# Running mean of the tokens on TensorE, phase biases as rows of a product, reciprocal of the positions first

## What is computed

```python
off_in = concatenate([x, pp], -1)                     # x: 4 x 512 x 64, pp: 512 x 32 phases
ao = (gelu(off_in @ hop_w1 + hop_b1) @ hop_w2 + hop_b2).reshape(B, L, H, P + 1)
center = tanh(ao[..., :P]) * PI                       # H = 4, P = 32
key_ph = tanh(x @ cpe_w + cpe_b) * PI
ctx = cumsum(x @ kce_w + kce_b, axis=1)
pos = arange(1, L + 1).reshape(1, L, 1)
storage_in = concatenate([x, ctx / pos], -1)          # ctx / pos: the running mean
st_ph = tanh(gelu(storage_in @ ksk_w1 + ksk_b1) @ ksk_w2 + ksk_b2) * PI
```

## Time and profile before

| | |
|---|---|
| median of 3 runs | 214.59 us (214.52 to 216.08) |
| the profiled execution's own time | 213.43 us |
| its span, first to last instruction | 211.7 us |
| TensorE products busy | 147.7 us (70%) |
| VectorE busy | 131.1 us (62%) |
| ScalarE busy | 73.9 us (35%) |
| GpSimd busy | 35.6 us (17%) |
| share of the chain that ended last | TensorE 43%, VectorE 34% |
| mean granted TensorE clock | 0.778 |

### The profile page before, as it was taken

How to read it: one execution, slowest core, us unless ns; L and a number is a source line. 1 busy time by engine, 2 the same in 40 slices (tenths; PEclk the granted TensorE clock), 3 DMA queues, 4 the chain that set the end, 5 groups by cost and what they waited for, 6 DMA issues and landing times.

```text
span 211.7 us, 2099 instructions
## 1 busy us (share of the span) xinstructions
PE 147.7 (70%) x690; PEld 90.8 (43%) x690; DVE 131.1 (62%) x342; ACT 73.9 (35%) x122; POOL 35.6 (17%) x52
## 2 busy tenths in 40 slices
PE   0889858029279694499581054877479989979992
PEld 0543524024175512458561053766454454534340
DVE  2659995789942898998879995388673005101011
ACT  2010511252233640784840230323063462444541
POOL 2031500346000472241402330000000000000000
PEclk9999979758857955558997555799555896799998
DMA  5999600000000000000000000000000000101011
GB/s 145 345 386 377 262 5 25 0 0 0 0 0 0 0 0 0 0 5 2 0 0 5 0 0 0 0 5 0 0 0 0 0 3 0 25 0 25 0 25 25
DMA packets 7042, 8.80 MB, mean 42 GB/s; under 512 B 2388, under 2 KB 4436, under 8 KB 7032
## 3 DMA queue, kind: packets, MB, share of 16 engines
q1 hardware_dynamic: 7032, 8.68, 12.2%
HBM read 8.15 MB, written 0.52 MB: 41 GB/s over the span
## 4 chain that ended last, share of the span: by engine, by line
PE 43%; DVE 34%; issue 9%; DMA 5%; ACT 5%; POOL 2%; SPq 1%; DVEq 0%; POOLq 0%; ACTq 0%
PE bank L900 8%; PE bank L884 6%; DMA dist_sb<-in_dist 5%; PE bank L885 4%; PE bank L861 2%; PE bank L640 2%; DVE dist_sb L988 2%; PE bank L705 2%; PE bank L698 2%; PE bank L702 2%; DVE proj L1059 2%; PE bank L707 2%; DVE invpos L993 2%; PE bank L690 2%; PE bank L754 1%
## 5 line engine op out<-in xcount | busy, mean ns | idle before, releaser
L586 ACT ACTIVATE hid<-bank 128x512 f32<-128x512 f32 x32 | 18.1, 596 | 23.3 <-PE bank L885 22.2
L900 PE MATMUL bank<-hid,ffn_sb 128*64 128x512 f32 x64 | 18.9, 676 | 0.0
L1271 DVE TENSOR_TENSOR h<-bank,h 128x256 f32<-128x256 f32 x4 | 1.7, 425 | 27.0 <-PE bank L909 27.0
L884 PE MATMUL bank<-xp,w1hi 128*128 128x512 f32 x32 | 16.6, 520 | 1.0 <-ACT xp L570 1.0
L885 PE MATMUL bank<-xp,w1lo 96*128 96x512 f32 x32 | 14.6, 455 | 0.0
L884 PEld LDWEIGHTS bank<-xp,w1hi 128*128 128x128 f32 x32 | 7.0, 220 | 14.4 <-ACT hid L586 8.1
L988 DVE TENSOR_TENSOR dist_sb<-dist_sb,mask_in 128x1024 f32<-128x1024 f32 x8 | 9.5, 1232 | 4.0 <-POOL mask_in L325 4.0
L698 PE MATMUL bank<-late_sb,proj 128*128 128x8 f32 x16 | 3.7, 364 | 10.8 <-ACT proj L469 10.8
L656 PE MATMUL bank<-early_sb,vk 128*128 128x128 f32 x8 | 2.2, 435 | 12.9 <-DVE vk L1038 12.9
L830 PE MATMUL bank<-early_sb,sq_c 128*128 128x2 f32 x16 | 2.9, 304 | 11.8 <-ACT sq_c L545 11.8
L640 PE MATMUL bank<-dist_sb,neigh 128*64 128x512 f32 x32 | 11.1, 775 | 0.0
(11 more groups left out here) (246 smaller groups left out, 369.4 us busy)
## 6 DMA issues: line engine op xcount, KB each, us to landing
dist_sb<-in_dist SPq DMA_DIRECT2D x4, 1024.0 KB, 10.8
mask_in<-in_mask SPq DMA_DIRECT2D x4, 256.0 KB, 10.0
ffn_sb<-in_ffn SPq DMA_DIRECT2D x1, 813.0 KB, 10.9
fold_sb<-in_folded SPq DMA_DIRECT2D x1, 772.0 KB, 12.1
late_sb<-in_late SPq DMA_DIRECT2D x1, 728.5 KB, 11.6
out<-h SPq DMA_DIRECT2D x8, 64.0 KB, 1.7
early_sb<-in_early SPq DMA_DIRECT2D x1, 391.0 KB, 3.2
mask_in<-in_mrows SPq DMA_DIRECT2D x1, 128.0 KB, 2.4
```

The lines of the kernel that those rows point to most:

```text
L586: nc.scalar.activation(hid[:, at % HB], bank[hid_bank[at % 3]][:, :], ACT.Gelu).then_inc(S["hid_set"], 1)
L884: nc.tensor.matmul(o, w1hi[:, e * HID:(e + 1) * HID], xp1[g][:, toks], start=True, stop=False)
L900: mm = nc.tensor.matmul(bank[2][j * D:(j + 1) * D, :], K["e_w2"][:, (e + j) * D:(e + j + 1) * D], hid[:, (at + j) % HB], start=False, stop ...
```

## The change

It makes the running mean on TensorE. A constant `run_mean` (128 x 4 x 128) holds, for each chunk c of 128 tokens, 1/position where the row's token is not later than the column's, and 0 elsewhere; GpSimd cuts it from `invpos` by an affine_select. cx is then summed in bank 3 straight from x, without its transpose: for each chunk c a product of x with the triangle of its own 128 columns, and one with `invpos` for all later columns (384, 256 and 128 of them). ScalarE copies the bank to cx. The scan and the multiply are gone. The biases of `center` and `st` become a product: a row of ones against a row of the bias, rounded to F32R in one row and its rest in another (rows 0 and 32 of 33), added in the bank in front of the fp32 product. ScalarE's tanh reads the banks, and three adds on VectorE per group are gone. The positions are written first and VectorE takes their reciprocal as its first instruction. GpSimd's two adds on x wait for the running mean. Banks 3 and 0 of the joint products change places. The late constants are shorter by one row block.

```diff
@@ gpsimd
+            nc.gpsimd.iota(invpos[:, :], [[1, L]], base=1, channel_multiplier=0,
+                           allow_small_or_imprecise_dtypes=True).then_inc(S["pos_set"], 1)
             nc.gpsimd.memset(ones[:, :], 1.0).then_inc(S["ones_set"], 1)
...
+            pool.wait_ge(S["inv_set"], 1)
+            nc.gpsimd.affine_select(out=run_mean[:], in_=invpos[:, :].rearrange("p (c t) -> p c t", t=P), compare_op=ALU.is_ge,
+                                    fill=0.0, base=0, pattern=[[0, NC], [1, P]],
+                                    channel_multiplier=-1).then_inc(S["run_set"], 1)
...
                 pool.wait_ge(S["x_set"], g + 1)
-                pool.wait_ge(S["xt_mm"], g + 1)
+                pool.wait_ge(S["cx_mm"], g + 1)
                 nc.gpsimd.tensor_tensor(v8(x[:, g]), v8(h[:, g]), v8(x[:, g]), ALU.add).then_inc(pool_step, 1)
@@ scalar, project
                 nc.scalar.copy(x_t[:, :], bank[0][:, :]).then_inc(S["xt_set"], 1)
                 yield
+                act.wait_ge(S["cx_mm"], g + 1)
+                nc.scalar.copy(cx[:, :], bank[3][:, :]).then_inc(S["cx_set"], 1)
                 act.wait_ge(S["hop_mm"], g + 1)
...
                 for k in range(2):
-                    act.wait_ge(S["center_set"], 2 * g + k + 1)
-                    half = flat(t_c[:, g, 4 * k:4 * k + 4])
-                    nc.scalar.activation(half, half, ACT.Tanh).then_inc(S["center_tanh"], 1)
+                    act.wait_ge(S["center_mm"], 2 * g + k + 1)
+                    nc.scalar.activation(flat(t_c[:, g, 4 * k:4 * k + 4]), bank[2 + k][:, :],
+                                         ACT.Tanh).then_inc(S["center_tanh"], 1)
                 yield
-                act.wait_ge(S["st_set"], g + 1)
-                nc.scalar.activation(kph[:, g, 1], kph[:, g, 1], ACT.Tanh).then_inc(S["st_tanh"], 1)
+                act.wait_ge(S["st_mm"], g + 1)
+                nc.scalar.activation(flat(kph[:, g, 1]), bank[1][:, 0:256], ACT.Tanh).then_inc(S["st_tanh"], 1)
@@ scalar, weights
+                act.wait_ge(late_in, 16)
+                nc.scalar.copy(ones_r[:, :], ones[0:ROWS, :]).then_inc(S["rows_hi"], 1)
+                nc.scalar.copy(bias_r[:, :], K["phase_rows"]).then_inc(S["rows_hi"], 1)
@@ tensor, project
+                def running(c):
+                    mm = nc.tensor.matmul(bank[3][:, c * P:(c + 1) * P], pair(x[:, g], c), run_mean[:, c, :],
+                                          start=(c == 0), stop=(c == NC - 1), skip_group_check=True)
+                    if c < NC - 1:
+                        mm = nc.tensor.matmul(bank[3][:, (c + 1) * P:L], pair(x[:, g], c), invpos[:, (c + 1) * P:L],
+                                              start=(c == 0), stop=False, skip_group_check=True)
+                    return mm
+
+                pe.wait_ge(S["run_set"], 1)
+                if g:
+                    pe.wait_ge(S["center_tanh"], 2 * g)
+                running(0)
                 pe.wait_ge(S["xt_set"], g + 1)
                 if g:
-                    pe.wait_ge(S["st_set"], g)
+                    pe.wait_ge(S["st_tanh"], g)
                 nc.tensor.matmul(bank[1][:, :], K["hop1x_bd"], x_t[:, :], start=True, stop=False)
...
+                for c in range(1, NC):
+                    mm = running(c)
+                mm.then_inc(S["cx_mm"], 1)
                 pe.wait_ge(S["fold_set"], 1)
...
-                joint(0, 3)
-                joint(1, 0)
+                joint(0, 0)
+                pe.wait_ge(S["cx_set"], g + 1)
+                joint(1, 3)
                 yield
...
                 def center(k, i):
+                    rows = bias_r[:, 0:P].unsqueeze(1).broadcast_to([ROWS, 2, P])
                     for c in (0, 1):
+                        half = bank[i][:, c * 256:(c + 1) * 256]
+                        nc.tensor.matmul(half, ones_r[:, :], rows, start=True, stop=False)
+                        mm = nc.tensor.matmul(half, hop_g[:, (2 * k + c) * P:(2 * k + c + 1) * P], K["hop2c_bd"],
+                                              start=False, stop=True)
...
                 center(0, 2)
-                pe.wait_ge(S["vk_set"], NC * g + 3)
+                pe.wait_ge(S["vk_set"], NC * g + 4)
                 center(1, 3)
...
                 for c in range(NC):
+                    part = bank[1][:, c * 64:(c + 1) * 64]
+                    nc.tensor.matmul(part, ones_r[:, :], rows, start=True, stop=False)
+                    mm = nc.tensor.matmul(part, ksk_g[:, c * P:(c + 1) * P], K["ksk2_bd"], start=False, stop=True)
@@ vector
             def tok_tables():
+                dve.wait_ge(S["pos_set"], 1)
+                nc.vector.reciprocal(invpos[:, :], invpos[:, :]).then_inc(S["inv_set"], 1)
...
             def constants():
                 dve.wait_ge(S["ones_set"], 5)
-                link(nc.vector.reciprocal(invpos[:, :], invpos[:, :]))
...
             def project(g):
-                dve.wait_ge(late_in, 16)
-                dve.wait_ge(S["xt_set"], g + 1)
-                if g:
-                    dve.wait_ge(S["ksk_mm"], g)
-                link(nc.vector.tensor_tensor_scan(cx[:, :], ones[:, :], x_t[:, :], 0.0, ALU.mult, ALU.add))
-                nc.vector.tensor_tensor(cx[:, :], cx[:, :], invpos[:, :], ALU.mult).then_inc(S["cx_set"], 1)
                 yield
...
-                for k, i in ((0, 2), (1, 3)):
-                    dve.wait_ge(S["center_mm"], 2 * g + k + 1)
-                    nc.vector.tensor_tensor(t_c[:, g, 4 * k:4 * k + 4], bank[i][:, :].rearrange("p (t q) -> p t q", q=P),
-                                            rows_bc(K["hop_b2c"], 4), ALU.add).then_inc(S["center_set"], 1)
-                yield
-                dve.wait_ge(S["st_mm"], g + 1)
-                nc.vector.tensor_tensor(kph[:, g, 1], bank[1][:, 0:256].rearrange("p (t q) -> p t q", q=PH),
-                                        rows_bc(K["ksk_b2"], 8), ALU.add).then_inc(S["st_set"], 1)
+                yield
                 dve.wait_ge(S["gate_mm"], g + 1)
...
             def weights(g):
+                low = slice(ROWS - 1, ROWS)
+                dve.wait_ge(S["rows_hi"], 2)
+                nc.vector.tensor_tensor(bias_r[low, :], K["phase_rows"][low, :], bias_r[low, :].bitcast(F32),
+                                        ALU.subtract).then_inc(S["rows_lo"], 1)
                 dve.wait_ge(ffn_in, 32)
```

## The result

The changed kernel took 218.47 us, the median of 4 runs (218.20 to 219.04), against 214.56 us for the kernel before (4 runs, 213.88 to 216.08). The ratio is 1.018, with a 95% interval of 1.012 to 1.024: it is slower by 1.8%. The profiled execution took 219.04 us, its span is 217.2 us, 5.5 us over the 211.7 of before, and its mean granted clock 0.775 (before 0.778).

A forecast was written before the change was run, and what follows sets the result against it. No single engine was the bound: a chain of waits passed between engines, through VectorE's running mean. Terms -1.3 - 0.5 - 2.2 - 0.1 = -4.1 took 213.43 to 209.3; the median's 1.16 offset made 210.5 us, range 207.8 to 213.5.

The forecast's parts named there:

- Reciprocal: Kernel start, VectorE: taking the reciprocal first brings group 0's variance earlier, -0.4 us, bounds 0 and -0.4.
- Group 0's release: TensorE's first product behind group 0's hop Gelu: comes at 58.1 us, a gain of 1.3 us including the reciprocal's 0.4.
- Clock kept in group 0: Group 0's eight small products on TensorE: the first finds the clock at the upper level, worth 0.5 us, between 0 and 3.
- Bias products: TensorE, center and st: eight per group at 0.2 and 0.12 us each, in all +1.3 us per group.
- Clock in group 1: Group 1's project stage: clock above 0.9 between 73 and 79 us, running mean at 79.25, about 2.2 us gained.
- The first rival: Group 1: the clock falls as before, so VectorE's saving is lost to TensorE; -2.0, 212.5 us, chance 0.25.
- End of project and tail: End of group 1's project and next queries: freed VectorE steps against 1.3 us of bias products, -0.1 us, between +1 and -1.
- The slow one: Third rival: TensorE at the lower clock level in 49 to 73 us, +6.5, 221.1 us, chance 0.10.
- The condition for being wrong: Running products over 2.95 us a group, clock 0.50 again at 73 to 82, or a bias pair costing like an fp32 one.

## Why the prediction was wrong

It named 210.5 us in a range of 207.8 to 213.5 and gave 0.10 to slower; 218.47 came. Step by step:

**Reciprocal.** It runs at 1.49 us for 3.35, as said. The variance of group 0 starts at 24.47, 1.2 us earlier instead of 0.4: the forecast took the Square in front of it as fixed at 24.65, and it moved to 23.83. Alone, at the end, it brings nothing that shows (0.998).

**Group 0's release: right, in part by luck.** 58.22 against 58.1, with the 2.03 us from table load to release to the hundredth (56.19 to 58.22). The way there differed by errors that cancel: the first running product started at 48.81 and not at 49.55, and the clock was low for it and the next (0.76 in 49 to 54). At the upper level a 128 column product takes 0.22 and one of 256 takes 0.44, under my 0.34 and 0.47.

**Clock kept in group 0: right in sign, too small.** The eight small products are at 1.06 us for 1.87 and the ksk products too: 3.2 us where I took 0.5 and gave 3 as the bound.

**Bias products: the step that failed.** I took 0.2 and 0.12 us, 1.3 per group, and let the price lie between 0 and that of the fp32 product, arguing by passes. They cost 0.51 (0.94 less 0.43) and 0.38 (0.59 less 0.21), 3.6 us per group at the upper level, more even than the bound (2.9, from my 0.47 and 0.25, which are busy times divided by four and hold the tail of the last product). At the lower level a pair is 1.66 and a st pair 0.97, in all 10.5 us for the eight pairs of group 1; the center and st products of group 0 before took 2.6 from start to start at the upper level. The cause is not the passes: at 65, 97 and 128 rows the same product costs 0.12, 1.0 us per group, under the 1.3 forecast. It is that eight products of 33 rows stand between products of 128 rows, and the weight load of each no longer runs under the product in front of it. In group 0 this ate the lead of 4.5 us at the center products nearly whole.

**Clock in group 1: half right where forecast, wrong behind it.** I wanted over 0.9 between 73 and 79; it was 0.81, at 0.50 from 72 to 74 and at 1.00 only from about 75.5 on, then to 92. The first rival's 0.50 in 73 to 82 did not come. The transposes decide nothing here, as the clock was down before they began; with bias products 128 rows deep it was 1.00 in 58 to 72, the transposes at 68.06 included. The forecast's times for group 1 leave out the 1.8 us that group 0 gained and add them only in the sum. With them taken off, it had the running mean at 77.45 and the argument at 80.5; they came at 79.5 and 77.50. GpSimd's adds began at 79.65 and missed the argument, and the absolute value of kph, beside no GpSimd work now, takes 0.42 us instead of 2.29. The release had gained 5.3 us by then, where the sum had 1.8 + 2.2 = 4.0. What I had not followed is what a faster TensorE meets next: the ksk Gelu, queued on ScalarE behind group 0's sines, holds it for 3.95 us, and half a microsecond behind that gap the clock falls, just when the dear pairs begin.

**End of project and tail.** I took -0.1, between +1 and -1. The VectorE step behind the gate read is at 0.17 us, as said, against 2.07; but the gate read itself is 2.5 us late, outside the bounds, since the 1.3 us of bias products became 8.4 us of longer stretch. By the run with bias products alone, 3.5 of these are the price at the upper level; the other 4.9, an estimate, are what the same products cost more at the lower one.

**The rivals.** The slow one ended near the right number (221.1) for a wrong reason: it put TensorE at the lower level in 49 to 73, where the clock was 0.86. The condition for being wrong, that a bias pair costs like an fp32 one, is the one that was met.

With the bias step at its measured price of 3.6 us per group instead of 1.3, and the rest as forecast, the sum would be 210.5 + 2 x 2.3 = 215.1: no change. The two traces show where the 5.5 us arose:

| start, us | before | changed | difference |
|---|---|---|---|
| first small product, group 0 | 59.43 | 58.22 | -1.2 |
| first center product or pair, group 0 | 67.64 | 63.18 | -4.5 |
| gate read, group 0 | 71.85 | 71.58 | -0.3 |
| first small product, group 1 | 87.43 | 82.16 | -5.3 |
| first center product or pair, group 1 | 97.85 | 92.01 | -5.8 |
| gate read, group 1 | 101.46 | 103.98 | +2.5 |
| xhl split | 145.02 | 150.57 | +5.5 |

The two stretches with the bias products lose 4.2 and 8.4 us, all else up to there gains, and the last 3.0 us are lost behind the gate read, where the clock is 0.50 in 100 to 112 for 1.00. The forecast had nothing for that last part. Nor was the rest of its sum right: with pairs at 0.55 us, less than it allowed, the kernels with 65 and 97 rows take 204.9 and 204.2 us, below the 207.8 at which its range began. Apart from the bias products it was too cautious by some 5 us.

## What to carry to other kernels

A short helper product between full ones is not priced by its columns or passes alone: look whether its own weight load still runs under the product in front of it, and if the helper is shallow, try it deeper with rows of zeros, or fewer and wider; here padding 33 rows to 65 turned a loss of 1.8% into a gain of 4.8%. When an edit makes one engine faster, follow it to its next wait and ask what clock it finds behind it. And a wait that moves work of GpSimd moves it beside other steps of VectorE, where a step of 0.2 us can become one of 1.3.

## What the runs showed of the hardware

A one-pass product 33 rows deep and 256 columns wide, between products 128 rows deep, adds 0.51 us at the upper clock level; 65, 97 and 128 rows deep it adds 0.12. Where between 33 and 65 the step lies was not tried. In fp32 the 33 row product made its neighbour dearer too (0.63 for 0.43). A product of 32 rows and 512 columns in fp32 cost its neighbours about 0.2 in all. A subtraction of a single row of 160 elements on VectorE took 2.06 us beside GpSimd's w1lo (2.35 us), and no run has it without GpSimd. Steps of 8 and 40 elements took 1.28 and 1.22 beside GpSimd's adds; apart from them they take 0.17 and 0.20.
